# Two attentions' first loads, constant rows and maxima moved beside the preceding token phase

## What is computed

```python
# first attention (8 heads of 32), over channels-normalised x
q, k, v = split(w_qkv @ (norm(x) * gamma))
sim = (q.T @ k) * 32**-0.5 + bias           # bias: a table over relative positions, per head
x = w_out @ (softmax(sim) @ v) + x
# second attention, with relative embeddings
t = tokens(x);  q, k, v = split(norm(t) @ W + b)
weights = softmax((q @ k.T + q @ emb[i - j]) / sqrt(32))
t = t + weights @ v
# then an expert layer with Sinkhorn gates and top-k routing
```

## Time and profile before

| | us |
|---|---|
| median of three runs | 3010.18 |
| the profiled execution | 3011.54 |
| its span | 3009.7 |

### The profile page before, as it was taken

One profiled execution on the slowest core, in us unless ns is written; L12 is line 12 of the kernel. 1 busy time (PEld: TensorE's weight loads), 2 busy tenths in 40 slices (PEclk: granted clock), 3 DMA queues, 4 the chain that ended last, 5 costly groups with the idle time before them and its releaser, 6 DMA issues. The chain is left out here.

```text
span 3009.7 us, 47639 instructions
## 1 busy us (share of the span) xinstructions
PE 2552.4 (85%) x18726; PEld 870.6 (29%) x18726; DVE 2007.4 (67%) x2966; ACT 1397.6 (46%) x2549; POOL 1985.7 (66%) x770
## 2 busy tenths in 40 slices
PE   5686799999999999969994999999999999961356
PEld 1454122222222222225551222222222222240235
DVE  3344677777777777757774777777777777758324
ACT  3233355555555555533331555555555555550012
POOL 0113488888888887854443878888888878850673
PEclk8798799999999999989996999999999999975558
DMA  2975113221231212226765312232123221170237
GB/s 51 210 251 172 40 47 78 58 50 47 57 78 47 50 47 73 63 95 214 238 207 156 72 47 60 77 75 60 46 60 99 54 60 47 46 253 14 76 113 260
DMA packets 239568, 289.43 MB, mean 96 GB/s; under 512 B 65014, under 2 KB 172790, under 8 KB 236006
## 3 DMA queue, kind: packets, MB, share of 16 engines
q1 hardware_dynamic: 196528, 259.08, 31.2%
q0 software_dynamic: 6144, 16.85, 1.8%
q10 hardware_dynamic: 36672, 10.45, 1.5%
HBM read 176.55 MB, written 111.57 MB: 96 GB/s over the span
## 5 line engine op out<-in xcount | busy, mean ns | idle before, releaser
L1300 POOL TENSOR_TENSOR bias<-bias 128x2048 f32<-128x2048 f32 x160 | 724.6, 4529 | 167.0 <-ACT bias L1272 153.1
L1090 DVE TENSOR_REDUCE row_min_kf<-PS 128x1 f32<-128x1024 f32 x532 | 625.8, 1219 | 289.8 <-PE PS L1082 288.2
L746 DVE CUSTOM_DVE_ANT_0 PS<-PS,bias 128x1024 f32<-128x1024 f32 x532 | 645.6, 1245 | 197.0 <-PE PS L734 195.5
L942 ACT ACTIVATE prob_af<-PS 128x512 f32<-128x512 f32 x1024 | 555.7, 595 | 416.6 <-PE PS L864 416.6
L1272 ACT ACTIVATE bias<-PS 128x512 f32<-128x512 f32 x1024 | 557.2, 597 | 412.5 <-PE PS L1198 411.3
L970 POOL TENSOR_TENSOR acc_af<-acc_af,prob_af 128x2048 f32<-128x2048 f32 x128 | 581.3, 4541 | 52.7 <-ACT prob_af L942 38.9
L1198 PE MATMUL PS<-stacks_kf 128*128 128x512 f16 x2048 | 533.2, 383 | 2.6 <-PEq L84 2.4
L857 PE MATMUL PS<-QS_af,KS_af 128*128 128x512 f16 x1024 | 329.6, 387 | 10.0 <-PEq L84 3.3
L1198 PEld LDWEIGHTS PS<-stacks_kf 128*128 128x128 f16 x2048 | 156.9, 97 | 443.6 <-ACT bias L1272 292.2
L890 PE MATMUL PS<-prob_af,V_af 128*32 128x512 f32 x2048 | 273.6, 606 | 0.3 <-ACT prob_af L942 0.3
L1218 PE MATMUL PS<-bias,V_kf 128*32 128x512 f32 x2048 | 272.7, 604 | 0.0
(11 more groups left out here) (183 smaller groups left out, 2943.2 us busy)
## 6 DMA issues: line engine op xcount, KB each, us to landing
stacks_kf<-query_key_halves SPq DMA_DIRECT2D x119, 256.0 KB, 7.1
query_key_halves<-stg SPq DMA_DIRECT2D x32, 768.0 KB, 3.8
xin<-in_x SPq DMA_DIRECT2D x32, 512.0 KB, 6.0
query_key_halves<-stg SPq DMA_DIRECT2D x32, 512.0 KB, 3.7
values<-vst SPq DMA_DIRECT2D x32, 512.0 KB, 4.1
KS_af<-query_key_halves SPq DMA_DIRECT2D x51, 256.0 KB, 4.8
QS_af<-query_key_halves SPq DMA_DIRECT2D x51, 256.0 KB, 6.9
V_kf<-values SPq DMA_DIRECT2D x9, 1024.0 KB, 10.6
```

The costliest lines, as they stand in the source:

```text
L746: nc.vector.tensor_tensor_reduce(out=max_ps[n % 2], in0=max_ps[n % 2], in1=bias[:, g * HG + j, z:z + N], scale=-1.0, scalar=3.0e38, op0=AL ...
L942: nc.scalar.activation(prob[:, n % PR, head, :], score_ps[s % 3], ACT.Exp).then_inc(exps, 1)
L1090: nc.vector.tensor_reduce(row_min[:, m:m + 1], max_ps[n % 2], AX.X, ALU.min).then_inc(max_read, 1)
L1300: nc.gpsimd.tensor_tensor(acc[:, u % 2], so_far, prob[:, n % PR], ALU.add).then_inc(acc_ok, 1)
```

## The change

1. Each attention becomes a generator. It sets up its tiles and yields a bundle (`Early`) before its loop; the main program passes the bundle to the token phase ahead, and runs the loop afterwards. The prologue blocks are gone.
2. Inside the token phase, SP issues the embedding tables at u = 0 (`load_tables`, second attention), the first group and values at u = 2 (`load_tokens`, behind waits for the stores of chunks 0 and 1), and moves the maxima at u = 14. At the end it waits for all of them.
3. POOL fills the constant rows at the start of the token phase, as f32 words where it can, in one memset for both slots in the first attention.
4. The 21 early maxima are put into `order` as "max" entries, `PER` = 2 a step from u = 4: in phase 0 behind the transposes and behind `bc`, in phase 1 behind the fourth `qk` product and behind `bc`. They use one pair of banks, 6 and 7 (`early_ps`), so each product waits for the reduction before it. In phase 0 VectorE waits for the bias windows ahead of the first.
5. The token phase's ring of banks shrinks from 8 to 6, `xh` and `xl` from three to two deep, and its large tiles lie in the attention's own memory (`rooms`).
6. In the first attention's loop VectorE copies the sums out of the bank (`take_sums`) and takes the reciprocal in place in SBUF in four pieces, one in each of the steps 2 to 5, ahead of the step's late maxima. POOL's `finish` waits for the fourth.

```diff
-        def token_phase(kind):
+        Early = namedtuple("Early", "rooms sems jobs after load_tables load_tokens fill product reduce move loaded")
+        def token_phase(kind, rooms, early):
...
+                RING = 6
+                jobs = list(enumerate(early.jobs))
+                PER = -(-len(jobs) // (NCH - early.after - 1))
...
+                    some = [("max", n, job) for n, job in jobs[:PER]] if u > early.after else []
+                    jobs = jobs[len(some):]
+                    for n, name in enumerate(steps):
+                        order.append(name)
+                        if some and n % (len(steps) // PER) == len(steps) // PER - 1:
+                            order.append(some.pop(0))
+                    order += some
...
-                    return PS[:, at[name] % 8, :]
+                    return PS[:, at[name] % RING, :]
...
+                            if u == 0:
+                                early.load_tables(sp)
+                            if u == early.after - 1:
+                                for n in range(NC):
+                                    sp.wait_ge(*is_stored(n))
+                                    sp.wait_ge(v_stored[n % 2], 16)
+                                early.load_tokens(sp)
+                            if u == NCH - 2:
+                                early.move(sp)
...
+                        early.loaded(sp)
...
+                            if what == "max":
+                                early.product(pe, u, m)
+                                continue
                             n = at[name]
-                            if n >= 8:
-                                pe.wait_ge(*read_out(order[n - 8]))
+                            if n >= RING:
+                                pe.wait_ge(*read_out(ring[n - RING]))
...
-                            if c >= 3:
-                                act.wait_ge(full, at[("v", c - 3, NV - 1)] + 1)
-                            nc.scalar.copy(xh[:, c % 3], xn[:, c % 2]).then_inc(high, 1)
+                            if c >= 2:
+                                act.wait_ge(full, at[("v", c - 2, NV - 1)] + 1)
+                            nc.scalar.copy(xh[:, c % 2], xn[:, c % 2]).then_inc(high, 1)
...
+                        early.fill(pool)
...
+                            if what == "max":
+                                if u == 0 and kind == 0:
+                                    dve.wait_ge(bias_in, 16 * ROWS)
+                                early.reduce(dve, u, m)
+                                continue
...
+                early_ps = [PS[:, 6:8, :].rearrange("p a n -> p (a n)")]
...
-                with nc.Block() as block:
-                    @block.sync
-                    def _(sp):
-                        load_group(sp, 0, 0, 0)
-                        load_values(sp, 0, 0, 0)
-                        sp.wait_ge(stk0, LOADS)
-                        sp.wait_ge(v_in0, 16)
-                        sp.wait_ge(mir_in, 64)
-                        sp.wait_ge(fill, 7)
-                        move_maxima(sp, 0, MJ)
-                        sp.wait_ge(m_in0, 16 * HG)
...
+                def fill_rows(pool):
+                    for n, (t_, value) in enumerate(((den_w[:], 1.0), (words(KS[LEAD:P]), 0.0), (words(QS_[LEAD:P]), 0.0),
+                                                     (KS[LEAD:LEAD + 1], 1.0))):
+                        nc.gpsimd.memset(t_, value).then_inc(fill, 1)
+                        pool.wait_ge(fill, n + 1)
...
+                def first_product(pe, n, job):
+                    if n == 0:
                         pe.wait_ge(stk0, LOADS)
+                    max_products(pe, n, job[0], job[1:], early_ps)
...
+                yield Early((room[:, :],), sems, singles, 3, lambda sp: None, load_tokens, fill_rows, first_product, first_reduce,
+                            first_move, all_loaded)
...
-                                pool.wait_ge(max_read, job_at[(u, "den")] + 1)
+                                pool.wait_ge(recd, PIECES * (u + 1))
...
-                                nc.vector.reciprocal(rec[:, u % 2, :], max_ps[n % 2][:, 0:CH]).then_inc(max_read, 1)
+                                nc.vector.tensor_copy(rec[:, u % 2, :], max_ps[n % 2][:, 0:CH]).then_inc(max_read, 1)
+                            def reciprocal(u, piece):
+                                dve.wait_ge(max_read, job_at[(u, "den")] + 1)
+                                c = slice(piece * CH // PIECES, (piece + 1) * CH // PIECES)
+                                nc.vector.reciprocal(rec[:, u % 2, c], rec[:, u % 2, c]).then_inc(recd, 1)
...
+                            for n in range(NU * KTU + DEN + 1 + PIECES):
+                                if n < len(early_jobs):
+                                    do(early_jobs[n])
+                                u, piece = n // KTU - 1, n % KTU - DEN - 1
+                                if u >= 0 and 0 <= piece < PIECES:
+                                    reciprocal(u, piece)
+                                if n < len(late_jobs):
+                                    do(late_jobs[n])
...
-        token_phase(0)
-        attention_first()
-        turned.close()
-        token_phase(1)
-        attention_keys_first()
+        for kind, attention in enumerate((attention_first, attention_keys_first)):
+            stages = attention()
+            early = next(stages)
+            token_phase(kind, early.rooms, early)
+            next(stages, None)
+            if kind == 0:
+                turned.close()
```

More of the change, by code:

```diff
@@ L2 @@
 from concourse import mybir
+from collections import namedtuple
 from contextlib import ExitStack
@@ L295, in tile, with roomy @@
                     return es.enter_context(nc.sbuf_tensor(f"{name}_{kind}", shape, dt))
+                used = [0] * len(rooms)
+                def roomy(words, dt, axes, **sizes):
+                    i = [u + words <= r.shape[1] for u, r in zip(used, rooms)].index(True)
+                    flat = rooms[i][:, used[i]:used[i] + words]
+                    used[i] += words
+                    return (flat if dt is F32 else flat.bitcast(dt)).rearrange(axes, **sizes)
                 NQ = (2 * G, 3 * G)[kind]
@@ L337, in token_phase @@
                     last_qk = NQ - 1
-                    order += (qk[0:2] + tp + qk[2:] + v[0:1] + bc + v[1:],
+                    steps = (qk[0:2] + tp + qk[2:] + v[0:1] + bc + v[1:],
                               qk[0:3] + proj + qk[3:last_qk] + tp + qk[last_qk:] + v[0:1] + bc + v[1:])[kind]
-                at = {n: i for i, n in enumerate(order)}
+                    some = [("max", n, job) for n, job in jobs[:PER]] if u > early.after else []
[5 more added lines that the diff above has]
+                    order += some
+                assert not jobs
+                at = {n: i for i, n in enumerate(n for n in order if n[0] != "max")}
+                ring = list(at)
                 def root_at(c):
@@ L442, in tokens_first @@
                                 for src, part in ((xh, 0), (xh, 1), (xl, 0)):
-                                    last = nc.tensor.matmul(out, src[:, u % 3, k, tok], wp[:, part, k, col:col + C],
+                                    last = nc.tensor.matmul(out, src[:, u % 2, k, tok], wp[:, part, k, col:col + C],
                                                             start=(n == 0), stop=(n == 3 * KT - 1))
@@ L476, in _ @@
                                 w, g = m % (NQ // G), m // (NQ // G)
-                                last = product(ps, wp, w * C + g * P, lambda s, k: (xh, xl)[s][:, u % 3, k, :])
+                                last = product(ps, wp, w * C + g * P, lambda s, k: (xh, xl)[s][:, u % 2, k, :])
                             else:
@@ L535, in split @@
                             pool.wait_ge(high, c + 1)
-                            nc.gpsimd.tensor_tensor(xl[:, c % 3], xn[:, c % 2], xh[:, c % 3], ALU.subtract).then_inc(low, 1)
+                            nc.gpsimd.tensor_tensor(xl[:, c % 2], xn[:, c % 2], xh[:, c % 2], ALU.subtract).then_inc(low, 1)
                         def add(s):
@@ L637, in _ @@
                                     op1=ALU.add).then_inc(vals, 1)
-                reset(sems)
+                reset(sems + early.sems)
         def attention_first():
@@ new lines, in load_tokens, with fill_rows @@
+                def load_tokens(sp):
+                    load_group(sp, 0, 0, 0)
+                    load_values(sp, 0, 0)
+                def fill_rows(pool):
+                    zeros = [(words(stacks[LEAD:P, q, st]), 0.0) for q in range(2) for st in (QL, KH1)]
+                    ones_ = [(stacks[LEAD:LEAD + 1, q, KH1], W1S * W1S) for q in range(2)]
+                    for n, (t_, value) in enumerate([(den_w[:], 1.0)] + zeros + ones_):
+                        nc.gpsimd.memset(t_, value).then_inc(fill, 1)
+                        pool.wait_ge(fill, n + 1)
```

182 lines of the change are left out of this document (87 added, 95 removed).

## The result

The changed kernel takes 2946.1 us (median of four runs, 2944.6 to 2948.5) against 3011.1 us for the kernel before on the same chip: ratio 0.9786, 95% interval 0.9773 to 0.9798. The forecast was 2956 us in a range of 2930 to 2980. The gain is 65 us where 54.4 were forecast.

What follows compares the result with a forecast made beforehand. The prediction took TensorE, busy 85% of the span, as the bound, with the prologues as its low stretches. Gains of 21.3 + 30.1 + 3 = 54.4 us off the 3010.2 us median gave 2956 us, range 2930 to 2980.

Steps and rivals of the forecast that it cites:

- The prologues: Stretches ahead of the two attention loops: 46.2 and 45.9 us removed in full, with nothing counted for the clock.
- Token phase 0: Phase ahead of the first attention: loads and reductions cost 15.9, 8.7 and 0.3 us of the 46.2, leaving 21.3 us gained.
- Rival (b): Token phase 0: the loads find room and the bias window lands about as before; 2943 us, chance 0.12.
- Token phase 1: Phase ahead of the second attention: maxima cost 14.8 us and loads 1 us of the 45.9, leaving 30.1 us gained.
- Rival (c): Token phase 1: its 20 us of loads stall PE there as they did alone; 2976 us, chance 0.15.
- The maxima: Early maxima in the token phases: two a step cost 1.09 us in phase 0 and 1.46 us in phase 1.
- The constant rows: Fills on POOL at the token phases' start: 14.1 us each, ending by POOL's first low part, so they cost nothing.
- the ring: Token phases: six banks instead of eight cost nothing, a bank being asked for again over 5 us later.
- The first attention's loop: Copying the sums and four reciprocal pieces: 0.13 us a unit gained over 31 units, net 3 us, bounds -6 and 22.
- Rival (a): First attention's loop: pieces cost much less from SBUF, under 0.65 us, so the full 0.73 us stays; 2937 us, chance 0.13.
- (d): Token phases: the maxima are not hidden, each a chain of product, reduction, product; 2980 us at least, chance 0.05.
- (e): First attention's loop, steps 2 to 5: every piece pushes the next product, +2.1 us a unit; 3025 us, chance 0.05.

## Why the prediction was right, and where it was not

The total came out inside the range, but by the prediction's own signs one part failed: it called itself wrong if the unit moved by more than 0.5 us, and it moved by 0.56.

**The prologues.** Right: their 46.2 and 45.9 us are gone and nothing came in their place. The first loop's scores follow the last values' store by 3.8 us (304.95 after 301.12), the second's by 5.7 (1577.24 after 1571.52), a little over the 5 foretold. Both loops start at a granted clock of 0.50 in both kernels, as forecast, yet the clock gave a little: it was at 1.00 some 5.4 and 2.9 us into the loops, before 7.8 and 6.0 (windows of 0.5 us). Half of the difference, 1.2 and 1.5 us, is the most that this can be worth (an estimate from these windows). The second loop and tail do not show it. The reading that both token phases keep PE at 94 to 100% holds for their steady parts: the whole of phase 0 has PE busy for 163.0 of 186.7 us, since it had a hole of its own for the bias windows.

**Token phase 0.** Right in its mechanism, which three kernels show. The walk through the queue had the first reduction at about 181 us (measured 181.55), step 5's eviction at 189.2 (189.60), step 6 at 199.9 (200.33), steps of 10.66 us (10.73). That the absolute times fit so well is in part luck, for two errors cancelled. The phase ran 2.0 us ahead of before when the hole came (value store of chunk 1 at 128.03, before 130.06), most of it because PE's clock rose at 105.5 us instead of 111.0. Counted from that store, step 6 begins 18.4 us late (72.3 against 53.9 us), not 15.9. Each later step cost 0.07 us more as well.

Rival (b), that the loads find room, was wrong for their place at step 2 and right for steps 4 to 6. The forecast took the queue's state at step 2 from ACT's waits; the same rows say that from 184 us there was room.

**Token phase 1.** Right: 1.56 us a step against 1.46 forecast (15.59 to 17.15), ten steps 15.6. Five steps where the loads run took 79.85 us against 77.93 (from one output projection on PE to the fifth behind it, 1319.34 to 1399.19, before 1356.25 to 1434.18), and one of them has its maxima already (1.56 us): the loads cost some 0.4 us, forecast 1. Rival (c) is out.

**The maxima.** A step's cost was rightly taken as the reduction that delays the reciprocal. The forecast priced the slots as given; it might have asked which slot costs least. Moved behind the value products, two a step, they cost 0.85 us a step in phase 1 and 0.94 in phase 0.

**The constant rows and the ring.** Both nothing, as forecast: the first with no margin at all in phase 0 (in phase 1 POOL still had 3.2 us to spare, its fills ending at 1304.49 and its first low part starting at 1307.70), the second within the 3 us that its interval leaves.

**The first attention's loop: the term that was mis-sized.** The mechanism was right in its first half: the bank is freed by a copy of 0.69 us, the 0.73 us of waiting go, and a part is given back. The forecast gave back 0.6 us of 0.73 and kept 0.13 a unit; measured are 0.56 kept, and the stage gained 17.5 us in place of 3. The part given back was mis-sized, and put down to the pieces, while what takes it back is, as read from the traces, a wait for ScalarE that the walk did not have. Nor did the waits ahead of (12,13) and (14,15) get longer, which the prediction had named as a sign: the first is 0.51 us in both kernels, the second does not show. The walk failed in three small places that all leaned one way. Counted from the (7,8) product at 376.23 as 0:
- The piece ahead of (12,13)'s reductions begins at 7.34 (383.57) and not at 7.49, because three chained reductions took 3.58 us from 379.99, not 3.68, and (9,10)'s began at 3.76, not 3.81. The trace of before has 3.58 us for the same three (402.37 to 405.95): the number was there to be read.
- A piece holds DVE for 0.86 us (383.57 to 384.43) and not for the 0.946 that its row gives as duration; the pair behind it takes 2.31 us and not 2.43. So (14,15) goes out at 10.71, forecast 10.95, before 10.37.
- The row maxima's transpose follows at 13.93 (390.16 - 376.23), before at 13.69. The delay of 0.34 us at (14,15) shrinks to 0.24 there, where the forecast wrote that the transpose takes no more from the delay; 0.24 us is what the ScalarE wait behind (7,8) had put in already. And the stretch that goes is 0.80 us (from the start of DVE's read of the sums to (7,8): 3.42 us before, 2.62 after) rather than the 0.73 read as a wait.

So 0.80 - 0.24 = 0.56 us a unit. Each misreading was 0.05 to 0.15 us, and the unit runs 31 times. The bounds of -6 to 22 held the result, the middle did not.

The kernel with one piece in place of four adds what the forecast did not ask: the gain stands on the pieces being small. The kernel with the moved piece shows that the second piece costs nothing where it is.

**Rival (a)** is out: the reciprocal from SBUF takes 948 ns, from the bank 946. The Trainium skill (VectorE: DVE Perf Modes, What auto-detection actually checks) would allow a faster rate for it between SBUF operands if the firmware enables that for the operation; this trace shows none. The loop gained nearly as much as this rival said, but not by its mechanism. **Rivals (d) and (e)** are out: the maxima are hidden but for 1.1 to 1.6 us a step, and no piece delays the unit by its end.

## What to carry to other kernels

Before moving loads into a running stage, look up when its queue runs free, and issue them in parts from there: here the same 13 transfers cost some 16 us at step 2, 7 at step 5, and next to nothing when spread over steps 4 to 6. Place a foreign product in a gap that PE already has and its reader behind what the gap waits for. Where a small difference is multiplied by the number of units, take the occupancy of chained instructions from the distance between their starts, and not from their listed durations, and walk every engine that the bottleneck waits for, not only the one that changes. Two gains measured apart need not add up: measure them together.

## What the runs showed of the hardware

- Chained instructions on DVE overlap at their ends: a reciprocal listed at 948 ns lets the next instruction start after 0.86 to 0.87 us (383.57 to 384.43 in after), and a whole one of 3.35 us after 3.27 (375.59 to 378.86 with one piece).
- A reciprocal of 128 x 128 f32 costs the same from SBUF (948 ns) as from PSUM (946 to 947 ns).
- A memset on POOL costs 0.84 to 0.86 ns an element a partition: 4096 words of 32 bits 3.51 us, 8192 of 16 bits 6.92 us, on one partition as on 32 (after, and the kernel with 16-bit fills).
- Removing a wait of TensorE uncovered the next one: of 0.80 us a unit, 0.24 went, as read from the traces, to a wait for ScalarE's exponential that had been covered.
- 2.75 MB of loads put into a full DMA queue ahead of a window that an engine waits for held the kernel for some 16 us; the same loads spread over three later steps for next to none.
